# Channel scaling, bias and residual addition of a quantized layer on GpSimd instead of VectorE

## The reference

```
x = x + sparse_attention(layernorm(x))          # sparsemax: needs each row of scores sorted
x = x + cross_attention(layernorm(x), ctx, mask)
x = x + quantized(layernorm(x))

def quantized(h):                               # per token
    scale = max(max(abs(h)), 1e-6) / 127
    q = clip(round(h / scale), -128, 127)       # int8
    return (q @ weight_q.T) * scale * weight_scale[None, :] + bias
```

## Time and profile before

| what | value |
|---|---|
| median of three runs | 3134.96 us |
| the profiled execution's own time | 3136.26 us |
| its span, first to last instruction | 3134.5 us |
| mean granted clock of TensorE | 0.887 of full speed |
| VectorE busy | 1995.2 us, 3935 instructions |
| GpSimd busy | 582.5 us, 565 instructions |
| the last stage's first scan behind which quant_add stands | at 2745.86 us |

### The profile page before, as it was taken

The page is one execution under the profiler, slowest core; times in us unless marked ns, Lnnn a source line. Parts: engine busy times, 40 slices in busy tenths (PEclk is TensorE's granted clock), DMA queues, the critical chain, the costliest instruction groups (busy, mean ns, idle before and its releaser), DMA issues. The chain is left out here.

```text
span 3134.5 us, 53684 instructions
## 1 busy us (share of the span) xinstructions
PE 2599.7 (83%) x20884; PEld 1494.5 (48%) x20884; DVE 1995.2 (64%) x3935; ACT 1468.9 (47%) x3051; POOL 582.5 (19%) x565
## 2 busy tenths in 40 slices
PE   6888889999599799979978998689979984657655
PEld 3555546666344344435544444455654642434433
DVE  7988745565587455557754543678872247887882
ACT  6676557777232132213334443278842323545543
POOL 1344311111000133324420000011113040000000
PEclk9999889999799899979988998789979995777766
DMA  1000010000000000010000000110011110000000
GB/s 61 2 2 2 2 40 4 8 8 1 4 1 0 32 2 2 1 43 12 12 5 1 0 1 19 43 54 9 8 54 43 39 54 4 11 21 21 14 17 7
DMA packets 41994, 51.98 MB, mean 17 GB/s; under 512 B 9291, under 2 KB 30868, under 8 KB 40724
## 3 DMA queue, kind: packets, MB, share of 16 engines
q1 hardware_dynamic: 39700, 44.39, 4.5%
q0 software_dynamic: 2048, 4.20, 0.5%
HBM read 39.39 MB, written 9.18 MB: 15 GB/s over the span
## 5 line engine op out<-in xcount | busy, mean ns | idle before, releaser
L130 POOL TENSOR_TENSOR l_rstd<-l_moments,const_minus_half 128x4 f32<-128x4 f32 x96 | 105.9, 1103 | 1401.9 <-DVE l_moments L124 1396.9
L1426 PE MATMUL l_p_gate<-l_h_t,w_wg 128*128 128x512 f32 x400 | 208.8, 604 | 0.0
L1449 PE MATMUL l_p_out<-l_hidden,w_wd 128*128 128x512 f32 x400 | 204.4, 594 | 2.6 <-DVE l_hidden L1719 2.5
L804 DVE TENSOR_REDUCE l_top<-l_ring 128x8 f32<-128x1024 f32 x128 | 150.9, 1221 | 79.4 <-PE l_ring L638 79.3
L2991 DVE SCALAR_TENSOR_TENSOR l_mix<-l_decay,l_cb 128x1024 f32<-128x1024 f32 x128 | 172.3, 1358 | 36.9 <-ACT l_decay L2869 35.9
L2869 ACT ACTIVATE l_decay<-l_p_ring 128x1024 f32<-128x1024 f32 x128 | 130.0, 1023 | 97.9 <-PE l_p_ring L2743 96.5
L350 ACT ACTIVATE l_probs<-l_probs,l_minus_top 128x128 f32<-128x128 f32 x512 | 156.8, 393 | 33.6 <-DVE l_minus_top L410 33.5
L1719 DVE TENSOR_TENSOR l_hidden<-l_act_out,l_p_spread 128x512 f32<-128x512 f32 x128 | 85.7, 685 | 128.6 <-ACT l_act_out L1547 128.3
L1209 DVE TENSOR_REDUCE l_minus_top<-l_p_score 128x4 f32<-128x1024 f32 x64 | 78.2, 1224 | 106.1 <-PE l_p_score L1037 102.5
L3647 DVE TENSOR_TENSOR l_srt<-l_srt 128x1024 f32<-128x1024 f32 (+3 forms) x112 | 115.7, 1033 | 27.0 <-ACT l_srt L3513 24.5
L753 ACT ACTIVATE l_probs_t<-l_ring 128x1024 f32<-128x1024 f32 x64 | 62.0, 1022 | 149.2 <-PE l_ring L662 149.2
(11 more groups left out here) (503 smaller groups left out, 6347.7 us busy)
## 6 DMA issues: line engine op xcount, KB each, us to landing
l_c_t<-in_ctx_t SPq DMA_DIRECT2D x24, 256.0 KB, 2.7
l_rows_in<-l_zero SPq DMA_DIRECT2D x1, 2432.0 KB
l_tile_h<-l_rows_in SPq DMA_DIRECT2D x38, 64.0 KB, 1.9
l_rows_out<-l_tile_y SPq DMA_DIRECT2D x38, 64.0 KB, 1.5
w_mask<-in_mask SPq DMA_DIRECT2D x1, 2048.0 KB, 9.2
w_wg<-in_l2f_wg SPq DMA_DIRECT2D x1, 2048.0 KB
w_wu<-in_l2f_wu SPq DMA_DIRECT2D x1, 2048.0 KB
w_wd<-in_l2f_wd SPq DMA_DIRECT2D x1, 2048.0 KB
```

What stands on the lines that cost most here:

```text
L130: return nc.gpsimd.tensor_tensor(rstd[:, :], moments[:, :, 1], minus_half[:, 0:moments.shape[1]], ALU.pow)
L804: nc.vector.tensor_reduce(top[:, b % 2, half * HALF:(half + 1) * HALF, 0], s, AX.X, ALU.max)\
L1426: nc.tensor.matmul(p_gate[k % 2][:, :], w["wg"][:, s, :], h_t[:, g % 4, :], start=True, stop=True)\
L1449: nc.tensor.matmul(p_out[:, :], w["wd"][:, s, :], hidden[:, k % 4, :], start=(s == 0), stop=(gated and s == steps - 1)).then_inc(down, 1)
```

## The change

The function `quant_add` moves from VectorE's program to GpSimd's. The three operations keep their order, operands and shapes. Between them GpSimd waits for a new semaphore `out_order`, where VectorE waited for its own. In GpSimd's loop the call stands first in the step, ahead of the powers of the normalizations. What waits for `added` and `quant_scaled` is the same as before; layer 0's code isn't touched.

```diff
+        out_order = L.sem("out_order")
...
-                def quant_add(k):
-                    dve.wait_ge(quant_scaled, k + 1)
-                    order.then(nc.vector.tensor_tensor(out8[:, :, :], out8[:, :, :], bcast(w["quant_scale"][:, :], [T, GROUP, D], 1),
-                                                       ALU.mult))
-                    order.then(nc.vector.tensor_tensor(out8[:, :, :], out8[:, :, :], bcast(w["quant_bias"][:, :], [T, GROUP, D], 1),
-                                                       ALU.add))
-                    nc.vector.tensor_tensor(rows_of(k), rows_of(k), out8[:, :, :], ALU.add).then_inc(added, 1)
...
-                    if (k := group_at(g, IN_QUANT + 9)) is not None:
-                        quant_add(k)
...
+                def quant_add(k):
+                    pool.wait_ge(quant_scaled, k + 1)
+                    nc.gpsimd.tensor_tensor(out8[:, :, :], out8[:, :, :], bcast(w["quant_scale"][:, :], [T, GROUP, D], 1),
+                                            ALU.mult).then_inc(out_order, 1)
+                    pool.wait_ge(out_order, 2 * k + 1)
+                    nc.gpsimd.tensor_tensor(out8[:, :, :], out8[:, :, :], bcast(w["quant_bias"][:, :], [T, GROUP, D], 1),
+                                            ALU.add).then_inc(out_order, 1)
+                    pool.wait_ge(out_order, 2 * k + 2)
+                    nc.gpsimd.tensor_tensor(rows_of(k), rows_of(k), out8[:, :, :], ALU.add).then_inc(added, 1)
+
                 for g in range(FIRST, END):
+                    if (k := group_at(g, IN_QUANT + 9)) is not None:
+                        quant_add(k)
                     if (k := group_at(g, BEFORE)) is not None:
                         norm_scale(SPARSE, k)
```

## The result

The changed kernel took 3126.52 us (median of 7 runs, 3120.75 to 3128.25) against 3135.42 us of the kernel before (7 runs). The ratio is 0.9965, with a 95% interval of 0.9953 to 0.9976. That is 11 us less by the ratio and 8.9 by the medians. The forecast was 3136.2 us, 1.2 more than before, in a range of 3130 to 3144.

The account below looks back on a forecast made before the run. VectorE was taken to bound the last layer at quant_add, though not everywhere. Gain 12.4 us, collisions 11.8 and tail 1.8 gave net +1.2 us: 3136.2 us against the median 3134.96, range 3130 to 3144.

Parts of the forecast that it names:

- Freed time on VectorE: Last layer, six groups with a scan in front: moving quant_add frees 2.06 us each, 12.4 us in all.
- Collisions: VectorE's offset or scan, and its inverse, wait on GpSimd's SBUF reads: 11 collisions of 1.07 us, 11.8 us lost.
- one collision for the fourth group: Fourth group: product ready only after the scan has started, so only the inverse is delayed, 1.07 us.
- That the scan holds GpSimd off: GpSimd's second operation waits through VectorE's scan, 4.4 us; assumed because the scan also reads two SBUF operands.
- The end: Eighth quant_add at the kernel's end: 3.95 us on GpSimd against 2.14 on VectorE, costing 1.8 us.
- The moved waits: Later offset, GpSimd's queue, SyncE's stores and ScalarE's scale_output waiting for `added`: all at nothing.
- Rivals 1 to 3: Last layer: one collision a group, 3130.8 us (18%); three in most groups, 3143.7 (16%); no contention, 3124.4 (7%).
- the rival without contention: Rival 3: GpSimd and VectorE don't delay each other in the last layer; -10.6 us, 3124.4 us, chance 7%.
- a shift of a microsecond may settle it otherwise, and I allow a few microseconds for that: Last layer's periods: a small shift may change TensorE's granted clock; allowance of a few microseconds around the forecast.
- The term for TensorE's granted clock: Last layer: no net change counted; 4% left for a clock shift larger than allowed for, half each way.
- The prediction's own sign of being wrong: Wrong if the scan is slowed throughout, not only at its start, or periods change length with TensorE's clock.
- Periods of the same work differ by 4.6 us: Last layer's full periods, 57.2 to 61.8 us: their spread was the basis for allowing a few microseconds.

Follow-up runs that it names:

- the end on VectorE: Changed kernel with the eighth quant_add back on VectorE, the first seven staying on GpSimd; 3126.82 us, ratio 0.9976.
- trimmed imitation: Kernel before without quant_add's three operations on any engine, with VectorE memsets of 800 and 661 elements imitating the hold-ups; 3124.37 us, ratio 0.9969.
- mimic: The untrimmed imitation: kernel before without quant_add's three operations, with VectorE memsets of 740 and 950 elements ahead of offset and inverse; 3128.78 us, ratio 0.9990.
- null: Kernel before, unchanged except for one empty line added; 3135.84 us, ratio 1.0000.
- after_small: Changed kernel with one 128x128 VectorE memset ahead of the threshold in every period, about 0.2 us each; 3129.58 us, ratio 0.9979.
- third set: Changed kernel measured a third time, unchanged, 11 runs; 3128.68 us, ratio 0.9981.
- behind the offset: Changed kernel with GpSimd's first operation also waiting for the cross attention's norm offset; 3132.86 us, ratio 0.9993.
- behind the inverse: Changed kernel with the eighth quant_add on VectorE and GpSimd's first operation also waiting for the inverse; 3131.97 us, ratio 0.9992.
- no_quant: Kernel before with quant_add's three operations left out on every engine, a one-element memset in their place; 3124.06 us, ratio 0.9969.
- the slowest: Changed kernel with GpSimd waiting for the offset and a 128x524 VectorE memset between offset and scan where GpSimd works; 3138.29 us, ratio 1.0013.

## Why the prediction was wrong

- **Freed time on VectorE**, 2.06 us in each of six groups: right. The three instructions are gone from the chain.
- **Collisions**: right in kind, place and order; 0.95 at the offset and 0.88 at the inverse instead of 1.07 each. I had one collision for the fourth group; it had two like the others, because its scaled product is ready 1.65 us before the scan there. Six groups cost 6 x 1.83 = 11.0 us instead of 11.8.
- **That the scan holds GpSimd off**: right. The second operation takes 5.33 us beside it. The rule of the Trainium skill (SBUF — State Buffer, who interferes with whom) that the prediction named is borne out by it.
- **The end**: +1.8 us, right. **The moved waits** cost nothing, right: ScalarE still stood idle for 7.35 us ahead of cross_top's result where it had 8.98.
- **The sum of these** is +0.4 us, where I had +1.2. Rivals 1 to 3 were all about this sum, and none of them happened. The measured 3126.5 lies nearest to the rival without contention, 3124.4, but the collisions of the forecast were all there: that nearness is chance.
- **What failed is the step "a shift of a microsecond may settle it otherwise, and I allow a few microseconds for that".** The term for TensorE's granted clock stood at zero with a few microseconds around it, and 4% for more. In the profiles it is 9.0 us, 7.2 from first sort to cross_add and 1.8 in one stretch behind it. The three ratios give -11.0, -4.1 and -6.0 us in all, so that with VectorE's +0.4 taken off the clock was worth about -4.5 to -11.4. The prediction's own sign of being wrong, periods that change length with TensorE's clock, is what came.
- **What I had in hand.** "Periods of the same work differ by 4.6 us" was misread: the window of 57.20 us has 230 matmuls where the others have 244. Those of the same work shown there are 58.86 and 61.84 us, 3.0 apart. Nor do the means of whole periods, 0.69 to 0.77, show the cost: the longest period has the highest, 0.77, while its stretch from first sort to cross_add has 0.67. I took the spread as noise around what the kernel costs, when it was a cost of the kernel that the change could take away.

What the runs show of the cause: the time is gained where TensorE decides, at a higher granted clock for the same matmuls, and GpSimd is not needed for it. The changed kernel has 23.04 us of VectorE's time from out-add over the scan to the first sort, where the kernel before has 23.28. In all three profiles of the changed kernel and in that with the end on VectorE the periods are 58.6 and 57.4 in turn, whatever the moment at which the stage began. The trimmed imitation, at 23.01 us and with nothing of quant_add on GpSimd, has the same first three periods and a ratio of 0.9969; the untrimmed one, at 23.23, has the uneven periods of the kernel before and 0.9990. So it is VectorE's timing that makes the difference, and not which engine does the work. This is shown by the two imitations.

That the length of VectorE's part alone decides is not shown, and some runs speak against it. At 23.23 to 23.31 us the five periods from the third to the last scan took 301.3 us (`mimic`), 299.2 (before), 298.9 (`null`) and 292.3 (`after_small`). The two pieces of VectorE's part differ between these kernels too, and the trimming changed both (+0.07 ahead of the scan, -0.29 behind it). A shorter part is no safe gain either: at 22.10 us the five periods took 295.7, at 23.04 only 289.0.

The runs' own clocks speak the same way: in the third set the kernel before has a mean granted clock of 0.8876 over 26 runs and the changed one 0.8895 over 11, and in each kernel the runs with more clock are the shorter ones (before: 3136.6 us at 0.887, 3130.7 at 0.889; changed: 3131.5 at 0.888, and one run of 3122.6 at 0.892).

What stays open: the exact pattern is seen in profiled executions only, which were the fastest of their sets in two of three sets of the changed kernel. How often the other runs have it can't be read. That they mostly have something like it is likely: over its 29 runs the changed kernel is 7.2 us below the means of the kernel before in the same sets, where the profiles have 9.5 from the third scan on. And I can't say from the runs by what rule the clock rises. The same VectorE timing gave one sequence in two different programs (behind the offset, behind the inverse), but two sequences in two executions of the kernel before.

The kernel with the end on VectorE measured 0.9976 where the changed kernel of the same set had 0.9987. The difference fits what its end saves, but the intervals overlap, and the first set of the changed kernel had 0.9965.

## What to carry to other kernels

When two engines trade work at nearly equal cost in a loop whose other part runs on TensorE with gaps, the direct sum is not the answer: read first the granted clock over the stretch in which the other engines wait for TensorE, not its mean over a period, and count the time at the low clock there as time that any small shift can give or take. Before such a gain is put down to the engine that does the work, imitate the timing with the work left where it was; and repeat the runs in several sets, because one set of seven was off by half of the effect.

## What the runs showed of the hardware that I had not expected

- VectorE's tensor_scalar over 128x4 elements with a single SBUF operand waited out a GpSimd operation (1.04 us instead of 0.17), while a tensor_reduce over 128x2048 beside two GpSimd operations kept its 2.29 us.
- The stretch between two engines' hand-overs can lengthen when the loop gets shorter: with 2.06 us a period off VectorE's part (`no_quant`), first sort to cross_add took 21.2 us and more, where the changed kernel has 18.8 and 19.9 in turn.
- Two programs that differ, but whose VectorE part of a period agrees to 0.01 us, showed periods that agree to 0.03 us, TensorE's granted clock included; two executions of the kernel before did not (58.86, 60.75, 60.55, 61.84 and 60.58, 61.99, 58.91, 61.22 us).
- The profiled time from the third scan to the end told more of a kernel's median than the whole span did: 374.9 us for the trimmed imitation (ratio 0.9969), 379.1 for the changed kernel (0.9965, 0.9987, 0.9981), 382.5 with 0.25 us more (0.9979), 386.4 behind the offset (0.9993), 388.6 for the kernel before, 389.2 for the slowest (1.0013). It is not exact: the untrimmed imitation has 388.8 and a ratio of 0.9990.
